# Routed experts on one core: the next block's first products issued ahead of a block's second ones

## The reference, cut to what matters

```
xe = normalized x (layer 2: times ln_g[e], plus ln_b[e])
h  = gelu(xe @ W1[e] + b1[e])
y  = h @ W2[e] + b2[e]
out = sum over the 2 chosen experts of weight * y
```

## Time and profile before

| | us |
|---|---|
| median of 3 timed runs | 9224.35 |
| lowest and highest of them | 9222.07, 9230.39 |
| span of the profiled execution | 9684.1 |
| TensorE busy in it | 6558.8 |
| POOL busy | 4253.2 |
| first stage, expert blocks | from 4796 to 5077 |
| second stage, expert blocks | from 6952 to 7456 |

### The profile page before, as it was taken

How to read it: one execution, slowest core, us unless ns; L and a number is a source line. 1 busy time by engine, 2 the same in 40 slices (tenths; PEclk the granted TensorE clock), 3 DMA queues, 4 the chain that set the end, 5 groups by cost and what they waited for, 6 DMA issues and landing times. The chain is left out here.

```text
span 9684.1 us, 146169 instructions
## 1 busy us (share of the span) xinstructions
PE 6558.8 (68%) x32929; PEld 4679.8 (48%) x32930; DVE 4925.4 (51%) x11606; ACT 2452.7 (25%) x6651; POOL 4253.2 (44%) x3778
## 2 busy tenths in 40 slices
PE   2266666646798777776585767776597566666698
PEld 2244444424465555554373555555486344444466
DVE  8633333334322777776516777777412444444433
ACT  0144433322221222222221222222222111111233
POOL 0078777760001666663042555554021466666000
PEclk9988878777898888888697888888699666766799
DMA  2299988880123666664144666665233333334000
GB/s 90 81 186 179 179 174 176 176 178 11 36 119 122 187 187 186 183 187 116 58 118 130 181 176 179 176 180 150 86 104 100 96 103 106 101 102 98 18 10 20
DMA packets 636665, 1221.72 MB, mean 126 GB/s; under 512 B 110509, under 2 KB 408077, under 8 KB 625556
## 3 DMA queue, kind: packets, MB, share of 16 engines
q0 software_dynamic: 311344, 725.84, 31.7%
q1 hardware_dynamic: 318660, 488.22, 16.4%
q10 hardware_dynamic: 6560, 6.55, 0.2%
HBM read 995.43 MB, written 224.77 MB: 126 GB/s over the span
## 5 line engine op out<-in xcount | busy, mean ns | idle before, releaser
L1827 POOL DMA_INDIRECT rows<-l_kv,index_staged x1728 | 1719.7, 995 | 1881.5 <-issue 706.0
L885 POOL DMA_INDIRECT gcn_sums<-out,target x806 | 1308.7, 1624 | 379.6 <-DMA gcn_sums<-out,target 168.4
L1933 PE MATMUL sum<-messages,hot 128*128 128x260 f32 (+1 forms) x3456 | 1136.7, 472 | 202.4 <-issue 89.3
L2671 POOL DMA_INDIRECT rows<-l_h,index_staged x864 | 919.1, 1064 | 529.8 <-issue 460.9
L1933 PEld LDWEIGHTS sum<-messages,hot 128*128 128x128 f32 x3456 | 728.9, 228 | 378.8 <-issue 184.3
L1910 PE MATMUL q<-queries,spread 128*128 x5184 | 773.7, 297 | 141.4 <-issue 75.8
L905 PE MATMUL g<-same,hot 128*128 128x128 f32 x1612 | 320.2, 375 | 611.9 <-DVEq L959 463.3
L2771 PE MATMUL sum<-messages,hot 128*128 128x259 f32 x1728 | 674.3, 547 | 79.7 <-DVE sums L2903 52.7
L1910 PEld LDWEIGHTS q<-queries,spread 128*128 128x128 bf16 x5184 | 527.6, 106 | 359.6 <-issue 220.2
L2061 DVE TENSOR_TENSOR rows<-q,rows 128x512 f32<-128x512 f32 x864 | 569.0, 683 | 174.9 <-DMA rows<-l_kv,index_staged 136.0
L905 PEld LDWEIGHTS g<-same,hot 128*128 128x128 f32 x1612 | 291.2, 278 | 714.0 <-issue 668.8
(11 more groups left out here) (443 smaller groups left out, 11302.3 us busy)
## 6 DMA issues: line engine op xcount, KB each, us to landing
window<-gcn_rows SPq DMA_DIRECT2D x806, 128.0 KB
rel<-slot_rel SPq DMA_DIRECT2D x324, 256.0 KB
l_kv<-stage SPq DMA_DIRECT2D x26, 2048.0 KB, 6.3
src_row<-in_src_row SPq DMA_DIRECT2D x62, 832.0 KB
first_part<-in_L_ffn_first SPq DMA_DIRECT2D x32, 1030.0 KB
rows<-l_kv,index_staged POOLq DMA_INDIRECT x1728
edge_attr<-in_attr SPq DMA_DIRECT2D x124, 208.0 KB
first_part<-in_L_ffn_first SPq DMA_DIRECT2D x32, 514.0 KB
```

What stands on the lines that cost most here:

```text
L885: pool.indirect_dma_start(out=copies[m], out_offset=bass.IndirectOffsetOnAxis(ap=target[:, u, j:j + 1], axis=0), in_=out[:, u, j, :], in_o ...
L1827: pool.indirect_dma_start(out=rows[:, u * 2 + n, j, :], out_offset=None, in_=table, in_offset=bass.IndirectOffsetOnAxis(ap=staged[:, u, n ...
L1933: ins = pe.matmul(sum_ps[g % 2][:, 0:W], hot[:, n, j, :], messages[:, n, j, :, :].rearrange("p h d -> p (h d)"), start=r == 0, stop=r == R ...
L2671: pool.indirect_dma_start(out=rows[:, u * 2 + n, j, :], out_offset=None, in_=table, in_offset=bass.IndirectOffsetOnAxis(ap=staged[:, u, n ...
```

## The change

TensorE's body is split. `units_of(s)` is the first products alone. Ahead of the loop TensorE turns block 0, runs its first products, turns block 1, and waits for the second weights. Then step s of the loop loads the expert's number of s, runs the first products of s+1, turns the rows of s+2, and runs the second products of s. `hid` gets two buffers. ScalarE waits for the second products of block s-2 rather than s-1. The start value of `unit_out` becomes `AHEAD` = C + 3. SP's load of block s waits until the Gelus of block s-2 are done, and increments a semaphore `loading` for which nobody waits. VectorE copies the rows of s+2 ahead of the results of s, and its wait for the second weights comes after the first two copies. POOL's program is the same.

```diff
     UNITS = 4
+    AHEAD = C + UNITS - 1
...
-        hid = ph.sb("hidden", [P, C, BLOCK])
+        hid = ph.sb("hidden", [P, 2, C, BLOCK])
...
             with eng.Fori(0, NB // 2 - 1) as i:
                 for u in range(2):
-                    body(i * 2 + u, u, i, True)
+                    body(i * 2 + u, u, i, 2)
             for u in range(2):
-                body(NB - 2 + u, u, NB // 2 - 1, u == 0)
+                body(NB - 2 + u, u, NB // 2 - 1, 1 - u)
...
-                def load(s, u, turn, more):
-
-                    sp.wait_ge(out_full, s * 2 + 2)
+                def load(s, u, turn, left):
+
+                    sp.wait_ge(unit_out, s * C + (UNITS - 1))
+                    sp.sem_inc(loading, 1)
                     e = expert_of(sp, reg, s)
...
-                def compute(s, u, turn, more):
+                def units_of(s, u, turn):
                     pe.wait_ge(xT_full, s + 1)
                     pe.wait_ge(w1_in[u], turn * 16 + 16)
                     for c in range(C):
 
-                        pe.wait_ge(unit_out, s * C + c)
+                        pe.wait_ge(unit_out, s * C + (c + C))
                         for kk in range(KK):
...
                         ins.then_inc(unit_full, 1)
-                    if more:
-                        turn_rows(s + 1, 1 - u, turn + u)
-                    pe.wait_ge(w2_in, 16 * (1 + E))
-                    pe.wait_ge(unit_out, s * C + (C + UNITS - 1))
+
+                def compute(s, u, turn, left):
                     e = expert_of(pe, reg, s)
+                    if left:
+                        units_of(s + 1, 1 - u, turn + u)
+                    if left > 1:
+                        turn_rows(s + 2, u, turn + 1)
+                    pe.wait_ge(unit_out, s * C + (C + AHEAD))
                     for h in range(2):
                         pe.wait_ge(out_out, s * 2 + (h + 1))
                         for c in range(C):
-                            ins = pe.matmul(outs[h][:, 0:D], hid[:, c, h * P:(h + 1) * P],
+                            ins = pe.matmul(outs[h][:, 0:D], hid[:, u, c, h * P:(h + 1) * P],
...
                 turn_rows(0, 0, 0)
+                units_of(0, 0, 0)
+                turn_rows(1, 1, 0)
+                pe.wait_ge(w2_in, 16 * (1 + E))
                 blocks(pe, compute)
...
-                act.sem_inc(unit_out, UNITS - 1)
-
-                def hidden(s, u, turn, more):
-                    act.wait_ge(out_full, s * 2 + 4)
+                act.sem_inc(unit_out, AHEAD)
+
+                def hidden(s, u, turn, left):
+                    act.wait_ge(out_full, s * 2 + 2)
...
-                def results(s, u, turn, more):
-                    if more:
-                        keep_rows(s + 1, 1 - u, turn + u)
+                def results(s, u, turn, left):
+                    if left > 1:
+                        keep_rows(s + 2, u, turn + 1)
                     dve.wait_ge(stored[u], turn * 32)
...
                 keep_rows(0, 0, 0)
+                keep_rows(1, 1, 0)
+                dve.wait_ge(w2_in, 16 * (1 + E))
                 blocks(dve, results)
```

More of the change, by code:

```diff
@@ L1468, in expert_blocks @@
         stored = [ph.sem(f"stored{u}") for u in range(2)]
-        turned, xT_full = ph.sem("turned"), ph.sem("xT_full")
+        turned, xT_full, loading = ph.sem("turned"), ph.sem("xT_full"), ph.sem("loading")
         unit_full, unit_out, out_full, out_out = (ph.sem(n) for n in ("unit_full", "unit_out", "out_full", "out_out"))
@@ L1564, in _ @@
             def _(act):
-                act.sem_inc(unit_out, UNITS - 1)
-                def hidden(s, u, turn, more):
-                    act.wait_ge(out_full, s * 2 + 4)
+                act.sem_inc(unit_out, AHEAD)
+                def hidden(s, u, turn, left):
+                    act.wait_ge(out_full, s * 2 + 2)
                     for c in range(C):
                         act.wait_ge(unit_full, s * C + (c + 1))
-                        act.activation(hid[:, c, :], units[c % UNITS][:, 0:BLOCK], ACT.Gelu,
+                        act.activation(hid[:, u, c, :], units[c % UNITS][:, 0:BLOCK], ACT.Gelu,
                                        bias=w1[:, u, d.bias_at + c:d.bias_at + c + 1]).then_inc(unit_out, 1)
@@ L1578, in _ @@
                 dve.sem_inc(out_out, 2)
-                dve.wait_ge(w2_in, 16 * (1 + E))
                 def keep_rows(s, u, turn):
```

## The result

The changed kernel takes 9273.48 us in the median of 4 runs (9264.25 to 9277.42), the kernel before 9224.17 (9222.07 to 9230.39): a ratio of 1.0047, 95% interval 1.0033 to 1.0062. It is slower by 49 us, where 58 were forecast. The profiled execution of the changed kernel is one of these runs, 9264.25, with a span of 9262.5.

The account below looks back on a forecast made before the run. TensorE was taken to bound both expert stages; first stage +87 us (waits for gathered rows and a slower clock), second -29, together +58 on 9224.35, giving 9282 us, range 9235 to 9345.

Parts of the forecast that it names:

- What is late next: First-stage transposes wait for gathers queued behind a scatter, starting at +6.5 us; TensorE idles 3.0 us in 29 blocks.
- The holes: TensorE's idle gap ahead of second products, 0.91 us a block in both stages, goes: 29 us in a stage.
- The clock: First stage: holes lower the granted clock to 8 tenths under transposes and second products, 1.0 us more, block 11.5.
- The slices that I went by: Profile-page slices with TensorE 7 tenths busy, as the first stage would be; their clock is mostly 8 tenths.
- a slow clock under the first products: First stage: said to be free, since the first products have 6.5 us.
- Late landing: Rival: weights and gathers meet, rows land after about 2.8 us; first-stage block 12.5, total +103, 9327 us; chance 0.12.
- Sum of the first stage: First stage: 29 x (11.5 - 8.39) = +90, three free blocks -3, together +87 us.
- three free blocks: First-stage blocks outside the 29 whose gather stands behind a scatter; counted as -3 us.
- The second stage: Holes go and rows land in time by 0.4 us behind first products of 6.91 us: -29 us.
- The weights: SP's load now waits for the Gelus of s-2, issued at +4.9 instead of +0.9; taken as costing nothing.
- The rival on the other side: POOL's chain is shorter without the profiler, so the kernel gets faster: -20 us, 9204; chance 0.09.
- The register load: TensorE's load of the expert's number, 0.75 us in the old hole, is covered by queued products and costs nothing.

Follow-up runs that it names:

- e1: Changed kernel with POOL issuing gather(s+3) instead of gather(s+2) ahead of scatter(s), into the same two buffers: 9177.88 us against 9245.75, ratio 0.9919.
- e8: Changed kernel with the empty slots of a block reading row p (their partition's number) instead of all row 0: 9263.00 us against 9245.51, ratio 1.0023.
- e5: Changed kernel, first-stage blocks loading only the last 16 weight columns (wrong expert's weights, only waits of use): 9293.62 us against 9245.51, ratio 1.0057.
- e6: Changed kernel with SP's wait put back, weights of block s loaded behind the second products of s-2, not its Gelus: 9656.81 us, ratio 1.0447.
- e9: Changed kernel with both the gather-order edit of e1 and the empty-slot edit of e8: 9629.82 us against 9708.13, ratio 0.9914.
- e10: Changed kernel again without an edit, on the chip of e9: 9768.33 us, ratio 1.0058 to the kernel before.
- e2: Kernel before with only POOL's gather order edited as in e1: 9245.73 us against 9245.75, ratio 0.9997.
- e7: Kernel of e1 with the read of the expert's number put back behind the wait for the Gelus: 9179.07 us, ratio 0.9934 to the kernel before.
- e3: Kernel before with TensorE reading the expert's number ahead of the transposes instead of behind the last Gelu's wait: 9217.99 us, ratio 0.9968.
- e4: Changed kernel with 11 small filler matmuls in the first stage ahead of the transposes that wait for rows: 9293.85 us against 9245.75, ratio 1.0048.

## Why the prediction was right

The time lies in the range, 9 us under the number, and the named cause is shown: e1 moves the gather in POOL's queue, and the loss turns into a gain. That the sum came so near is in part luck: in the first stage the clock was put 14 us and the block 9 us too high, and 13 us of late landing weren't in it.

- **What is late next.** The chain from the end of the second products was put at +6.5, of which the landing was 1.8 after the last issue, between ends of 1.3 and 3.8. Measured: 1.8 and +6.4 to +6.6 in 21 of 29 blocks. The estimate by "DMA: Bandwidth & Descriptors" of the Trainium skill (Anatomy of one DMA), 2.3 and +6.95, was 0.5 too long for these blocks.
- **The holes.** Put at 0.91 a block, measured 1.05: in e1, with nothing between them, transposes and second products take 0.54 + 3.35 = 3.89 us, where 0.57 + 3.46 = 4.03 was used. Behind a hole they take still less, 0.38 + 3.35 = 3.73 (4797.18 to 4800.91), so the ordinary block without the clock is 10.18 rather than 10.5. For the 29 blocks that is some 9 us less.
- **The clock.** This step failed in its form. A mean clock of 0.8 was put on every block, 1.0 us, 29 in all. The regular hole of 3.0 us costs nothing of the clock (80 us at 1.00, and e8's 0.99 without the stage's start); the fall comes in the late blocks, and in one block after the stage's start. What it costs is the 14.8 us by which the second products exceed e1's, 130.4 against 115.6 busy. The slices that I went by are 242 us long each, and average over holes of many lengths. That a slow clock under the first products would be free was off as well, since 2 x 3.46 is more than 6.5; it didn't matter, as they took 3.43 in each of these blocks.
- **Late landing.** It was a rival with a chance of 0.12 for all blocks. It came in eight of them, for 13 us, by a mechanism that the prediction doesn't have: it named the meeting of weights and gathers, and the cause that e8 shows is the empty slots, which the kernel's code clamps to row 0. e5 leaves the weights a part of it, about a third.
- **Sum of the first stage:** 29 x (6.45 + 3.73 - 8.39) = 52, late landing 13, clock 15, three free blocks -3: 77, against 78.5 measured and 87 forecast.
- **The second stage** was forecast at -29 and came at -28.2, by two errors against each other: the holes were worth 33 (as e1 shows), and late landing took 5 back, which e8 removes. It came in eight blocks there too, though not the same ones (5, 9, 14, 23, 25 and 29 to 31), 0.4 to 1.0 us each.
- **The weights.** That they cost an ordinary block nothing is shown by e5; that their load had to move is shown by e6.
- **The rival on the other side** is out by its premise. POOL's issues are as long in runs of either total: L1504 took 963 ns in the median in the profiled execution of 9684.1 and L1506 965 in that of 9262.5. The 5% is most likely the chip, which is argued and not shown: on the chip of e9 and e10 the kernel before takes 9708 in timed runs, the mean granted clock is 0.83 in its profiles as in that of before (0.847 or more in all others), and the first stage begins at 4820 and 4823 there, at 4802 in that of before, and at 4699 or earlier in all others. The stages had the same lengths as elsewhere (273.3 and 494.5; in e2, whose order costs nothing, 273.6 and 495.0).
- **The register load** costs nothing in the new order, as assumed, and e7 shows that the same holds for the late place. In the kernel before it was 0.47 of the 0.75 us that the prediction gave it (e3).

## What to carry to other kernels

When a step is moved ahead on one engine, follow everything it reads back through the other queues: an unchanged program on GpSimd that was a block early became just too late, because its gather stood behind a scatter that waits for the block in hand. Read the price of a wait from the order of the queue that the supplier stands in, not from the amount of work, and move the supplier by the same distance as the consumer. A register read behind a wait is worth moving ahead of it where that wait ends last (0.47 us a block in e3), and not where the wait has long been met (e7).

## What the runs showed of the hardware that was not expected

- A gather of 256 rows landed 1.8 us after its last issue, but 2.9 to 3.8 us after it in the eight blocks that e8 mends, where empty slots all name the same row; naming different rows brought all of them to 1.8 or so.
- Holes of 3.0 us in each 10 us left the granted clock at 1.00 for 80 us and more; after the holes of 4.2 us and more it fell to about 0.50 (1.2 GHz) in every such block of the changed kernel, and the second products took 4.9 to 5.2 instead of 3.32. But the length of the hole alone doesn't decide: holes of 4.0 (e10) and 4.4 (the last of e5) kept it, and it fell after the first hole of 3.1 in the stage, once more after a hole of 3.0 in e5, and after the 2.2 to 2.4 that small matmuls left of the hole in four late blocks of e4. What decides stays open.
- The same kernel takes 9224, 9246 or 9708 us on different chips, while the two stages of the experts, where TensorE or the chain through POOL is the bound, keep their lengths (changed kernel: 351.8 and 466.3 on one, 349.8 and 466.2 on another).
